# Scores of two units side by side on two row parts, keys kept once, and projections of one attention as 128 and 64 rows

## The chip, the cores and the metric

The kernel runs on one core of a Trainium2 chip. A core has five engines with queues of their own: TensorE (PE in the rows; its weight loads are listed as PEld), VectorE (DVE), ScalarE (ACT), GpSimd (POOL) and SyncE (SP), which here issues loads and stores. TensorE reads its operands from the on-chip memory (SBUF, 128 partitions) and writes to eight banks of PSUM, from which VectorE and ScalarE copy. The metric is the device time of one execution in microseconds; lower is better.

## What is computed

A model of several layers on 16 sequences of 102 tokens with 192 features, all in float32: tokens and words are embedded, then come attention 0 (with relative positions), a layer of slots, attention 1 behind a convolution, a routed expert layer, attention 2, an MLP, attention 3 and a second expert layer. The change bears on the attentions 0, 1 and 2, each with 12 heads. Attention 2 in the reference, with 64 features a head:

```python
x = layernorm(h)                                      # (16, 102, 192)
q, k, v = (split_heads(x @ w) for w in (w_q, w_k, w_v))   # each w: 192 x 768
scores = einsum('bhnd,bhmd->bhnm', q, k) / sqrt(64)
attn = softmax(scores, axis=-1)
h = h + merge_heads(einsum('bhnm,bhmd->bhnd', attn, v)) @ w_o + b_o
```

Attention 1 has queries, keys and values of 16 features a head. Attention 0 has queries and keys of 64 and values of 16, adds to the scores a product of the queries with position keys, shifted row by row, and divides alike.

## The kernel before

Each attention runs in four turns (a loop over NG = 4 groups of GB = 4 sequences). A turn first turns the normalized rows XN (`xt`, L1856 for its transposes) into XT, 96 features on the partitions in two parts; then come the projections to queries (QT), keys and values, and then the attention proper.

**Units.** A unit is three heads of one sequence; a turn has 16 units, and `attention` (L1905 and on, on TensorE) runs 23 steps. At step s TensorE does, in this order: the scores of unit s (L1929, three products of 102 x 102, into one bank), a third of an output projection of a finished sequence (L1941, in some steps from 10 on), the values of unit s - 5 (L1958), the transposes of the probabilities of unit s - 3 (L1968), and in attention 0 what stands beside (`pos`, position products L2019, or work of the next turn, L1856 and L2011).

**The round of a unit.** VectorE takes the minimum of the scores (L931; in attention 0 it first adds the positions, L925), ScalarE three exponentials with their sums (L1620), VectorE the reciprocals (L937), GpSimd the product of probabilities and reciprocals (L675), TensorE the transposes, ScalarE the copy to PT (L1614), TensorE the values, and when a bank of values is full VectorE copies it to OT (L947). VectorE's order at its step s is: the copy to OT of unit s - 6 if it filled a bank, the minimum of unit s, the reciprocals of unit s - 1. ScalarE's order is: PT of unit s - 4, exponentials of unit s, and in attention 0 what stands beside. A bank of values is full after two units in attention 2 and after four in the others.

**Banks.** Eight banks are dealt out by name. Outside attention 0, scores rotate over banks 0, 1 and 6 and values over 4 and 7; in attention 0, scores have 0 and 1 and values have 4, and 6 and 7 serve the work beside. A wait of TensorE for a bank of values is a wait for VectorE's copy to OT (`values_taken`).

**Keys in halves.** The scores use all 128 rows of a tile of QT, which holds the same three heads of two units (four in attention 1), one on each part of the rows. So that only one unit's rows count, KZ holds the keys once for each part with zeros in the other rows. GpSimd clears KZ ahead of each attention (L687, L762, L808), and ScalarE or VectorE copies each key tile in pieces: two of 64 rows in attention 0 (L1652 and L1653, or L1126 and L1127) and 2 (L1793, L1794), four of 32 rows in attention 1 (L1765).

**Projections of attention 2.** Each of 12 tiles of queries and keys and 8 of values is two products over 96 rows (`two`, `token_rows`, in `product`, L1838), with 408 columns for queries and keys (banks 6 and 7) and 384 for values (banks 4 and 5). Every float32 product shows as two records in the trace. VectorE normalizes the next turn's rows (`layernorm`, L881) while TensorE projects this one's.

## Time and profile before

| | us |
|---|---|
| median of three runs | 1664.0 (1656.38 to 1665.09) |
| the profiled execution, its own time | 1669.9 |
| its span | 1668.2 |
| TensorE busy in the span | 1421.3 |
| ScalarE busy | 657.6 |
| VectorE busy | 675.5 |
| GpSimd busy | 387.6 |

The profile is of one execution. A row of a time line gives the start in us from the start of the span, the length in us, the engine, the line of the kernel, the operation, what it writes and reads, and how many instructions were merged in the row; in brackets stands how long the engine was idle before it and what ended that. A matmul's length is more than its share of the engine, since matmuls are pipelined: starts are to be compared with starts. Attention 0 lies at 71 to 290 us, attention 1 at 633 to 815, attention 2 at 1052 to 1315.

### The profile page before, as it was taken

Reading aid. Unit: us, or ns where it says so; the run is one execution under the profiler, and the core shown is the slowest. Engines: PE = TensorE matmul, PEld = TensorE weight load, DVE = VectorE, ACT = ScalarE, POOL = GpSimd, SP = SyncE. Lnnn points to the kernel's source line nnn. Section 1 sums busy time; section 2 is a strip of 40 time slices with the busy share of each in tenths; the row PEclk is TensorE's granted clock in tenths of the full one; section 3 lists DMA queues with packets and bytes.
Section 4 is the critical chain, followed back from the end, with each engine's and each line's share of the span. In section 5 each row is a group of like instructions: output and inputs, shape, how many; then the busy total and the mean of one; then the engine's idle time right before and its main releaser. Section 6 shows DMA issues by size and latency. Waiting matters only on the chain.

```text
span 1668.2 us, 31119 instructions
## 1 busy us (share of the span) xinstructions
PE 1421.3 (85%) x10060; PEld 1047.2 (63%) x10060; DVE 675.5 (40%) x2110; ACT 657.6 (39%) x2225; POOL 387.6 (23%) x467
## 2 busy tenths in 40 slices
PE   5898887685678687888999899699999999989994
PEld 4556655552233355666668899375676776889994
DVE  5357667511101665444334422344343323451113
ACT  1477666230000335777642122255554542113331
POOL 5122223210000222222201365121121100024441
PEclk8699999567876698999999899799999999889997
DMA  7342432529996200000005464200000300136553
GB/s 221 92 130 72 129 86 73 232 92 417 415 416 208 77 1 1 1 0 0 1 0 142 147 197 147 67 2 0 0 0 0 133 0 0 41 96 189 186 170 106
DMA packets 98454, 178.71 MB, mean 107 GB/s; under 512 B 35434, under 2 KB 62344, under 8 KB 96720
## 3 DMA queue, kind: packets, MB, share of 16 engines
q1 hardware_dynamic: 84160, 130.65, 24.7%
q10 hardware_dynamic: 7056, 30.67, 4.5%
q0 software_dynamic: 7136, 16.10, 3.1%
q8 instruction: 56, 0.92, 0.2%
q14 instruction: 46, 0.38, 0.1%
HBM read 150.39 MB, written 26.99 MB: 106 GB/s over the span
## 4 chain that ended last, share of the span: by engine, by line
PE 58%; issue 12%; DVE 12%; DMA 8%; ACT 6%; SPq 2%; POOL 1%; DVEq 0%; ACTq 0%; POOLq 0%
PE bank L1838 15%; DMA WM<-in_fc 6%; PE bank L2355 6%; PE bank L2341 4%; PE bank L1929 4%; PE bank L1941 4%; PE bank L1958 3%; PE bank L2345 3%; PE bank L1968 3%; PE bank L2019 2%; PE bank L2011 2%; PE bank L1904 2%; ACT ON L1620 2%; PE bank L2272 2%; DVE MXU L931 1%
## 5 line engine op out<-in xcount | busy, mean ns | idle before, releaser
L1838 PE MATMUL bank<-XT,AREA 96*128 96x408 f32 (+1 forms) x640 | 240.4, 534 | 33.1 <-ACT XT L1574 15.8
L1838 PEld LDWEIGHTS bank<-XT,AREA 96*128 96x128 f32 (+1 forms) x640 | 122.4, 197 | 140.1 <-issue 100.8
L1929 PE MATMUL bank<-KZ,QT 128*102 128x102 f32 x1152 | 138.8, 259 | 8.7 <-ACT PB L1620 5.8
L675 POOL TENSOR_TENSOR PB<-PB,RCU 102x306 f32<-102x306 f32 x96 | 69.2, 720 | 329.4 <-DVE RCU L937 329.3
L659 POOL TENSOR_TENSOR RS<-VE,expo 102x4 f32<-102x4 f32 (+1 forms) x53 | 53.0, 1000 | 385.9 <-DVE VE L877 326.1
L1929 PEld LDWEIGHTS bank<-KZ,QT 128*102 128x102 f32 x1152 | 120.7, 172 | 26.3 <-issue 17.0
L2355 PE MATMUL bank<-WM,KZ 128*128 x660 | 118.2, 327 | 0.0
L2355 PEld LDWEIGHTS bank<-WM,KZ 128*128 128x128 f32 x660 | 105.7, 190 | 0.4
L1601 ACT ACTIVATE KZ<-bank,AREA 128x128 f32<-128x128 f32 x198 | 54.8, 376 | 121.7 <-PE bank L2345 121.7
L1958 PE MATMUL bank<-PT,VALL 102*32 102x102 f32 (+1 forms) x1152 | 85.3, 268 | 16.6 <-DVE OT L947 14.1
L1941 PE MATMUL bank<-AREA,OT 128*102 128x192 f32 x384 | 88.5, 344 | 11.1 <-DVE SLOTS L1292 5.3
L1614 ACT ACTIVATE PT<-bank 102x306 f32<-102x306 f32 x192 | 86.0, 450 | 26.2 <-PE bank L1968 25.7
L794 POOL DMA_INDIRECT rows_out<-KZ,TARGET x66 | 66.6, 1009 | 119.0 <-DVE KZ L1437 74.2
L675 POOL TENSOR_TENSOR ON<-ON,RCU 102x306 f32<-102x306 f32 x96 | 67.0, 698 | 90.8 <-DVE RCU L937 90.4
L1620 ACT ACTIVATE PB<-bank,MXU 102x102 f32<-102x102 f32 x192 | 65.8, 375 | 53.9 <-DVE MXU L931 53.8
L2341 PE MATMUL bank<-KZ,SLOTS 128*128 128x128 f32 x660 | 84.6, 275 | 2.6 <-issue 2.6
L2341 PEld LDWEIGHTS bank<-KZ,SLOTS 128*128 128x128 f32 x660 | 82.0, 192 | 3.4 <-issue 3.4
L1572 ACT ACTIVATE XT<-bank 96x408 f32<-96x408 f32 x56 | 25.9, 502 | 140.2 <-PE bank L1856 117.1
L782 POOL DMA_INDIRECT KZ<-rows_in,TOKEN x66 | 67.6, 1024 | 54.1 <-DVE TOKEN L1414 34.6
L931 DVE TENSOR_REDUCE MXU<-bank 102x3 f32<-102x306 f32 x128 | 61.0, 477 | 42.3 <-PE bank L1929 37.9
L1958 PEld LDWEIGHTS bank<-PT,VALL 102*32 102x32 f32 (+1 forms) x1152 | 43.1, 118 | 55.7 <-issue 33.9
L1838 PE MATMUL bank<-AREA,XT 96*102 96x192 f32 (+2 forms) x320 | 72.1, 377 | 0.0
(336 smaller groups left out, 2655.7 us busy)
## 6 DMA issues: line engine op xcount, KB each, us to landing
AREA<-in_fc SPq DMA_DIRECT2D x10, 1536.0 KB, 25.1
SLOTS<-in_m3w SPq DMA_DIRECT2D x33, 384.0 KB
WM<-in_fc ACTq DMA_DIRECT2D x5, 2304.0 KB, 14.0
WM<-in_fc SPq DMA_DIRECT2D x6, 1536.0 KB, 24.6
AREA<-in_fc ACTq DMA_DIRECT2D x4, 2304.0 KB, 14.4
SLOTS<-in_m1w SPq DMA_DIRECT2D x33, 256.0 KB
AREA<-pos_scratch SPq DMA_DIRECT2D x16, 459.0 KB
pos_scratch<-AREA SPq DMA_DIRECT2D x8, 913.5 KB
```

What stands on the lines that cost most here:

```text
L675: pool.tensor_tensor(p, p, scale, ALU.mult).then_inc(sem["probs_ready"], 1)
L782: pool.indirect_dma_start(XG[i % XRING], None, rows_in, bass.IndirectOffsetOnAxis(ap=TOKEN[:, i:i + 1], axis=0), bounds_check=NB * T - 1, ...
L794: pool.indirect_dma_start(rows_out, bass.IndirectOffsetOnAxis(ap=TARGET[:, i:i + 1], axis=0), YO[i % YRING], None, bounds_check=2 * NB * T ...
L931: give(dve.tensor_reduce(MXU[:, n % 4, 0:HPU], scores, AX.X, ALU.min), "probs_in")
L1614: free(activation(PT[s % 2][:, 0:HPU, :], src, ACT.Copy), k)
L1620: last = activation(p, p if pos else psum[k][0:T, cols(j)], ACT.Exp, scale=-1.0, bias=MXU[:, s % 4, j:j + 1], accum_out=SMU[:, s % 4, j:j ...
L1838: last = pe.matmul(dst, lhsT, rhs, start=n == 0, stop=n == len(pieces) - 1)
L1929: last = pe.matmul(psum[k][0:T, cols(j)], QT[:, tile, cols(bb)], KALL[:, unit % per_tile * (HEADS // per_tile) + tile, cols(bb)], start=Tr ...
L1941: last = pe.matmul(psum[PROJBANK][0:T, 0:D], OT[bb % 2][:, m, :], wo[:, m, :], start=m == 0, stop=m == parts - 1)
L1958: last = pe.matmul(psum[k][row:row + rows, cols(tile)], by_head(dv)[:, bb * HEADS + h, :], PT[n % 2][:, j, :], start=True, stop=True)
L2341: pe.matmul(p[:, c], w_all[:, (j * per + m) * 128:(j * per + m + 1) * 128], x[:, 0:TILE], start=m == 0, stop=False)
L2355: last = pe.matmul(p[:, 0:D], HG[i % HRING][:, f * 128:(f + 1) * 128], w2[:, bass.ds(e, 1), f * D:(f + 1) * D].rearrange("p o d -> p (o d) ...
```

## The change

**Scores.** At the end of every even step, behind values and transposes, TensorE computes the scores of units s and s + 1, their products in turns, one unit on one part of the rows and the other on the next (64 rows each in attentions 0 and 2, 32 in attention 1), into two banks. At odd steps there are none. Keys are kept once (KT); the pieces, the clearing of KZ and the waits for it are gone. Outside attention 0 the banks for scores are 0, 1, 6 and 7, those for values are bank 4 alone.

**Projections of attention 2.** The weights of queries, keys and values are loaded as 128 rows and, beneath, as the last 64 rows with one half of the columns on partitions 0 to 63 and the other on 64 to 127. VectorE writes the first 128 features of the normalized rows to XN and the last 64 twice side by side to TWICE, so that XT has 128 features in part 0 and the last 64 twice in part 1. Two tiles are made at a time: each gets a product over 128 rows and one over 64 rows, the two of 64 rows on different row parts, and from one pair of tiles to the next the order of 128 and 64 alternates. Queries and keys take four banks (2, 3, 6, 7), values four (0, 1, 4, 5). W2_LOADS becomes 20.

TensorE in the middle of attention 2, before (QT and KZ: queries and keys; PT: turned probabilities; OT: finished rows):

```order
L1958 MATMUL bank7<-PT0,VALL 64x102 [waits values_taken,bank_free2]
L1958 MATMUL bank7<-PT0,VALL 64x102 x2
L1968 MATMUL bank2<-ident,PB0 102x102 [waits bank_free2,probs_ready]
L1968 MATMUL bank2<-ident,PB0 102x102 x2
L1941 MATMUL bank5<-AREA,OT1 102x192 x2
L1958 MATMUL bank7<-PT1,VALL 64x102 [waits bank_free3]
L1958 MATMUL bank7<-PT1,VALL 64x102 x2
```

and the same place in the changed kernel, with scores in banks 6 and 7:

```order
L1965 MATMUL bank6<-KZ,QT 102x102 [waits exp_ready]
L1965 MATMUL bank7<-KZ,QT 102x102
L1965 MATMUL bank6<-KZ,QT 102x102
L1965 MATMUL bank7<-KZ,QT 102x102
L1965 MATMUL bank6<-KZ,QT 102x102
L1965 MATMUL bank7<-KZ,QT 102x102
L1996 MATMUL bank4<-PT0,VALL 64x102 [waits values_taken]
L1996 MATMUL bank4<-PT0,VALL 64x102 x2
L2006 MATMUL bank2<-ident,PB0 102x102 [waits bank_free2,probs_ready]
```

Scores now come by sixes ahead of the values of an odd step, and values go to bank 4 where they had 4 and 7 in turns.

VectorE in the changed kernel, around the copy to OT that those values wait for (its order is as before):

```order
L934 TENSOR_REDUCE MXU<-bank6 102x3 [waits scores_ready,sums_ready]
L940 RECIPROCAL RCU<-SMU 102x3 [waits exp_ready,probs_in]
L950 COPY OT0<-bank4 128x306 [waits values_ready,sums_ready]
L934 TENSOR_REDUCE MXU<-bank7 102x3 [waits scores_ready,values_taken]
L940 RECIPROCAL RCU<-SMU 102x3 [waits exp_ready,probs_in]
```

The copy stands between the minima of the two units of a pair.

The diff, cut to its core:

```diff
-W2_LOADS = 8 + 6
+W2_LOADS = 3 * 3 + 5 + 6
+SBANKS, TBANKS, OBANKS, XBANKS, FBANKS, VBANKS = (0, 1), (2, 3), (4, 5), (6, 7), (2, 3, 6, 7), (0, 1, 4, 5)
-        SCORES, VALUES = (SBANKS + XBANKS[:1], SBANKS), (OBANKS[:1] + XBANKS[1:], OBANKS[:1])
+        SCORES, VALUES = (SBANKS + XBANKS, SBANKS), (OBANKS[:1], OBANKS[:1])
...
-            pool.wait_ge(sem["gated"], at.now("gated") + CT3)
-            pool.wait_ge(sem["power_out"], at.now("power_out"))
-            pool.memset(KZ[:], 0.0).then_inc(sem["halves_cleared"], at.one("halves_cleared"))
-            pool.wait_ge(sem["halves_cleared"], at.now("halves_cleared"))
...
+            def layernorm_in_parts(src):
+                statistics(src)
+                power(ts(VE[:], MV[:, :, 1], EPS, None, ALU.add))
+                dve.wait_ge(sem["xn_taken"], at.now("xn_ready"))
+                for bb in range(GB):
+                    mean, scale = MV[:, bb, 0:1], RS[:, bb:bb + 1]
+                    ts(XN[:, bb, 0:128], src(bb)[:, 0:128], mean, scale, ALU.subtract, ALU.mult)
+                    last = ts(TWICE[:, bb, :].rearrange("t (two p) -> t two p", two=2),
+                              src(bb)[:, 128:D].unsqueeze(1).to_broadcast([T, 2, D - 128]),
+                              mean, scale, ALU.subtract, ALU.mult)
...
-                src = full(k)[:, 0:TG]
-                activation(KZ[0:64, 0, p, :], src[0:64], ACT.Identity, bias=bk0[0:64, p:p + 1])
-                free(activation(KZ[64:128, 1, p, :], src[64:128], ACT.Identity, bias=bk0[64:128, p:p + 1]), k)
+                free(activation(KT[:, p, :], full(k)[:, 0:TG], ACT.Identity, bias=bk0[:, p:p + 1]), k)
...
-                    src = full(k)[:, 0:TG]
-                    for u in range(UPB):
-                        rows = slice(32 * u, 32 * u + 32)
-                        last = activation(KALL[rows, 3 * u + j, :], src[rows], ACT.Identity,
-                                          bias=bqk1[rows, 3 + j:4 + j])
-                    free(last, k)
+                    free(activation(KT[:, j, :], full(k)[:, 0:TG], ACT.Identity, bias=bqk1[:, 3 + j:4 + j]), k)
...
+            def two_at_once(banks, shape, whole, half, n):
+                places = [claim(banks) for _ in range(2)]
+                last = [None, None]
+                for step in range(2):
+                    for j, (k, p) in enumerate(places):
+                        lhsT, rhs = (half if step == n % 2 else whole)(j)
+                        last[j] = pe.matmul(p[0:shape[0], 0:shape[1]], lhsT, rhs, start=step == 0, stop=step == 1)
+                        if step == 0 and j == 0:
+                            say_taken(last[j])
+                return [filled(ins, k) for ins, (k, p) in zip(last, places)]
...
-                for s in range(STEPS):
-                    if s < UNITS:
-                        bb, unit = s // UPB, s % UPB
-                        k = banks[s % len(banks)]
-                        if s < len(banks):
+                def scores_of_two(first):
+                    two_units = (first, first + 1)
+                    for n in two_units:
+                        if n < len(banks):
+                            k = banks[n]
                             pe.wait_ge(sem[f"bank_free{k}"], at.now(f"bank_full{k}") + 1)
                         else:
                             pe.wait_ge(sem[scores_read], at.take(scores_read))
-                        for j in range(HPU):
-                            tile = unit // per_tile * HPU + j
-                            last = pe.matmul(psum[k][0:T, cols(j)], QT[:, tile, cols(bb)],
-                                             KALL[:, unit % per_tile * (HEADS // per_tile) + tile, cols(bb)],
-                                             start=True, stop=True)
-                        last.then_inc(sem["scores_ready"], at.one("scores_ready"))
+                    for j in range(HPU):
+                        for n in two_units:
+                            bb, unit = n // UPB, n % UPB
+                            row = unit % per_tile * (128 // per_tile)
+                            rows, tile = slice(row, row + 128 // per_tile), unit // per_tile * HPU + j
+                            last = pe.matmul(psum[banks[n % len(banks)]][0:T, cols(j)], QT[rows, tile, cols(bb)],
+                                             KT[rows, tile, cols(bb)], start=True, stop=True)
+                            if j == HPU - 1:
+                                last.then_inc(sem["scores_ready"], at.one("scores_ready"))
...
+                    if s < UNITS and s % 2 == 0:
+                        scores_of_two(s)
...
-                xt()
+                xt_in_parts()
                 qk = []
-                for w in (wq2, wk2):
-                    for p6 in range(6):
-                        k, p = claim(XBANKS)
-                        qk.append(filled(product(p[:, 0:TG], two(w, p6 * 128, (p6 + 1) * 128)), k))
+                for n, w in enumerate((wq2, wk2)):
+                    for m in range(3):
+                        qk += tiles_at_once(w, m, 3 * n + m)
```

## Rows read from the trace of the kernel before

**Rows 1.** The page, part 1: busy us, share of the span, instructions.

```profile
PE 1421.3 (85%) x10060; PEld 1047.2 (63%) x10060; DVE 675.5 (40%) x2110; ACT 657.6 (39%) x2225; POOL 387.6 (23%) x467
```

**Rows 2.** Windows: a turn of attentions 0, 1, 2; PE, PEld, DVE, ACT, POOL busy, clock, DMA.

```profile
128.00:186.00 58.00, 51.49 (x412) 35.18 (x410) 41.69 (x111) 40.20 (x152) 13.92 (x18) 1.00 0.39 103
686.00:729.00 43.00, 37.74 (x312) 26.51 (x312) 18.88 (x58) 32.74 (x131) 12.15 (x17) 1.00 0.00 0
1126.00:1189.00 63.00, 59.78 (x379) 41.20 (x378) 26.84 (x74) 33.56 (x133) 12.15 (x17) 1.00 0.00 0
```

**Rows 3.** Time line of attention 2, TensorE and one minimum of VectorE.

```profile
1102.72 0.56 PE L1958 MATMUL bank<-PT,VALL 102*64 102x102 f32 x6
1103.22 0.47 PE L1968 MATMUL bank<-ident,PB 102*102 102x102 f32 x3
1103.53 0.70 PE L1929 MATMUL bank<-KZ,QT 128*102 128x102 f32 x6
1104.16 0.56 PE L1958 MATMUL bank<-PT,VALL 102*64 102x102 f32 x6
1104.34 0.48 DVE L931 TENSOR_REDUCE MXU<-bank 102x3 f32<-102x306 f32 x1
...
1105.51 0.82 PE L1941 MATMUL bank<-AREA,OT 128*102 128x192 f32 x4
1106.25 0.56 PE L1958 MATMUL bank<-PT,VALL 102*64 102x102 f32 x6
```

**Rows 4.** Time line of TensorE in the second expert layer.

```profile
1561.02 1.50 PE L2341 MATMUL bank<-KZ,SLOTS 128*128 128x128 f32 x12
1562.45 0.94 PE L2345 MATMUL bank<-KZ,SLOTS 64*128 64x128 f32 x12
1563.32 0.33 PE L2328 MATMUL bank<-ident,KZ 128*128 128x128 f32 x1
```

**Rows 5.** The chain of waits: start, us, what; the projections of attention 2.

```profile
1128.35 27.03 PE bank L1838 x80
```

**Rows 6.** Time line of attention 1: key copies and the first scores.

```profile
692.21 7.28 ACT L1765 ACTIVATE KZ<-bank,AREA 32x408 f32<-32x408 f32 x12 [0.77 <-PE bank L1838]
...
699.59 1.83 PE L1929 MATMUL bank<-KZ,QT 128*102 128x102 f32 x18 [0.67 <-issue]
```

**Rows 7.** Time line ahead of attention 1 and in its first turn.

```profile
633.02 5.24 DVE L881 TENSOR_SCALAR XN<-SLOTS,MV,RS 102x192 f32<-102x192 f32 x4 [1.12 <-POOL RS L659]
633.11 4.18 POOL L762 MEMSET KZ<- 128x4896 f32 x1
...
644.01 1.25 DVE L881 TENSOR_SCALAR XN<-SLOTS,MV,RS 102x192 f32 x4 [1.21 <-POOL RS L659]
```

**Rows 8.** Time line of attention 1: ScalarE and TensorE.

```profile
706.43 0.39 ACT L1620 ACTIVATE PB<-bank,MXU 102x102 f32<-102x102 f32 x1
...
706.64 0.38 PE L1958 MATMUL bank<-PT,VALL 102*32 102x102 f32 x6
...
707.39 0.49 ACT L1614 ACTIVATE PT<-bank 102x306 f32<-102x306 f32 x1
...
707.94 0.38 PE L1958 MATMUL bank<-PT,VALL 102*32 102x102 f32 x6
```

**Rows 9.** Attention 0: waits of PE (us in total, times, longest); time line around one.

```profile
PE bank L1958 <- DVE OT L947: 14.1, 8, 3.6
...
153.84 0.47 DVE L947 COPY OT<-bank 128x306 f32<-128x306 f32 x1
...
154.36 0.38 PE L1958 MATMUL bank<-PT,VALL 102*32 102x102 f32 x6 [0.61 <-DVE OT L947]
```

**Rows 10.** Time line of attention 0: scores of units 11 and 15, and position copies.

```profile
159.12 0.78 PE L1929 MATMUL bank<-KZ,QT 128*102 128x102 f32 x6
...
160.35 0.88 ACT L1662 ACTIVATE AREA<-bank 102x406 f32<-102x406 f32 x2
...
170.28 0.78 PE L1929 MATMUL bank<-KZ,QT 128*102 128x102 f32 x6
```

More of the change, by code:

```diff
@@ L375, in build @@
         a2(KD, 2, NB * T)
-        wq2, wk2, wv2 = a2(KD, 2, FF), a2(KD, 2, FF), a2(KD, 2, FF)
+        wq2, wk2, wv2 = ((a2(128, FF), a2(128, HALF_F)) for _ in range(3))
         wo2, bo2 = a2(128, 6, D), a2(T, D)
@@ L416, in build @@
                "second_loaded", "biases_loaded", "gelu_loaded",
-               "y_ready", *(f"y_loaded{g}" for g in range(NG)), "moe_done", "halves_cleared", "values_ready", "values_taken", "scaled",
+               "y_ready", *(f"y_loaded{g}" for g in range(NG)), "moe_done", "values_ready", "values_taken", "scaled",
                "attn0_done", "attn1_done",
@@ L684, in _ @@
             powers(1)
-            pool.wait_ge(sem["power_out"], at.now("power_out"))
-            for half in range(2):
-                pool.memset(KZ[64 - 64 * half:128 - 64 * half, half, :, :], 0.0
-                            ).then_inc(sem["halves_cleared"], at.one("halves_cleared"))
-            pool.wait_ge(sem["halves_cleared"], at.now("halves_cleared"))
             words(NB // 2, NB, "words_behind")
@@ L804, in _ @@
             expert_rows(1)
-            for r in range(YRING):
-                pool.wait_ge(sem[f"scattered{r}"], 16 * len(range(r, TILES, YRING)))
-            for half in range(2):
-                pool.memset(KZ[64 - 64 * half:128 - 64 * half, half, :, :], 0.0
-                            ).then_inc(sem["halves_cleared"], at.one("halves_cleared"))
-            pool.wait_ge(sem["halves_cleared"], at.now("halves_cleared"))
             powers(1)
@@ L886, in layernorm @@
                     step(last)
+            def layernorm_in_parts(src):
[8 more added lines that the diff above has]
+                              mean, scale, ALU.subtract, ALU.mult)
+                give(last, "xn_ready")
+                dve.wait_ge(sem["xn_ready"], at.now("xn_ready"))
             xn = lambda bb: XN[:, bb, :]
@@ L957, in attention, with values @@
                         between(s)
-            def values(v, dv, bias):
+            def values(v, dv, bias, banks=OBANKS):
                 per = 2 * D // dv
@@ L963, in values @@
                 for first in range(0, GB * HEADS, per):
-                    k = at.bank(OBANKS)
+                    k = at.bank(banks)
                     src = full(k)[0:T, 0:per * dv].rearrange("p (h d) -> p h d", d=dv)
@@ L1785, in _ @@
             with at.loop(act, NG) as g:
-                turned(XT)
-                for p in range(6):
-                    k = at.bank(XBANKS)
+                turned(XTALL)
+                for p in (0, 3, 1, 4, 2, 5):
+                    k = at.bank(FBANKS)
                     free(activation(QT[:, p, :], full(k)[:, 0:TG], ACT.Copy, scale=-0.125), k)
-                for p in range(6):
-                    k = at.bank(XBANKS)
-                    src = full(k)[:, 0:TG]
-                    activation(KZ[0:64, 0, p, :], src[0:64], ACT.Copy)
-                    free(activation(KZ[64:128, 1, p, :], src[64:128], ACT.Copy), k)
+                for p in (0, 3, 1, 4, 2, 5):
+                    k = at.bank(FBANKS)
+                    free(activation(KT[:, p, :], full(k)[:, 0:TG], ACT.Copy), k)
                 attention()
@@ L1871, in xt, with xt_in_parts, tiles_at_once, values_at_once @@
                 fresh.append(True)
+            def xt_in_parts():
+                pe.wait_ge(sem["xn_ready"], at.take("xn_ready"))
+                out = []
+                for part in (XN[:, :, 0:128], TWICE):
+                    k, p = claim(XBANKS)
+                    for bb in range(GB):
+                        last = pe.transpose(p[:, cols(bb)], part[:, bb, :], ident[0:T, 0:T])
+                    out.append(filled(last, k))
+                moved(*out)
+                fresh.append(True)
+            def two_at_once(banks, shape, whole, half, n):
[8 more added lines that the diff above has]
+                return [filled(ins, k) for ins, (k, p) in zip(last, places)]
+            def tiles_at_once(w, m, n):
+                whole, half = w
+                rows = lambda j: slice(64 * j, 64 * j + 64)
+                return two_at_once(FBANKS, (128, TG),
+                                   lambda j: (whole[:, j * HALF_F + m * 128:j * HALF_F + (m + 1) * 128], XTALL[:, 0, :]),
+                                   lambda j: (half[rows(j), m * 128:(m + 1) * 128], XTALL[rows(j), 1, :]), n)
+            def values_at_once(w, bb):
+                whole, half = w
+                rows = lambda j: slice(64 * j, 64 * j + 64)
+                return two_at_once(VBANKS, (T, HALF_F),
+                                   lambda j: (XTALL[:, 0, cols(bb)], whole[:, j * HALF_F:(j + 1) * HALF_F]),
+                                   lambda j: (XTALL[rows(j), 1, cols(bb)], half[rows(j), :]), bb)
             def two(w, n0, n1, x=XT):
@@ L2254, in _ @@
             convolution_out(1)
-            zeros_there(1)
             with at.loop(pe, NG) as g:
```

36 lines of the change are left out of this document (15 added, 21 removed).

## The prediction

> **What bounds the kernel now.** I read the page first [rows 1]: TensorE (PE) is busy for 85% of the span, ScalarE (ACT) for 39%. That is a mean over many stages, so I next cut out one turn of each of the three attentions [rows 2]. In attention 2 TensorE is busy for 60 of 63 us, in attention 1 for 38 of 43, in attention 0 for 51 of 58. ScalarE is busy for 34, 33 and 40. So attention 2 is bound by TensorE, attention 1 nearly as much by ScalarE, and attention 0 by both and the waits between them. Nothing else in the program is touched, so only these three stages (four turns each) and what stands ahead of them can move the time.
>
> Then the time line of TensorE for one unit of attention 2 [rows 3]. The reader is to see that the starts lie end to end: values 1102.72, transposes 1103.22, scores 1103.53, so 0.50, 0.31 and, up to the next values at 1104.16, 0.63: one unit in 1.44 us. An output projection adds 0.65, from 1105.51 to 1106.25 less the 0.09 by which scores end sooner where no values follow.
>
> **What the pairs save, part by part.** *Rows side by side.* The experts already run halves of 64 rows in pairs [rows 4]: twelve records of full rows take 1.43 us to the next line, twelve of 64 rows 0.87, the way back to full rows in it. For a change between full and part rows I take the 0.09 that scores show above when values follow. Scaled from 128 columns to 102, two units' scores cost 0.77 with both changes; I take 0.82, since the first weights of a block show. Before they cost 2 x 0.63. Gain on TensorE: 0.4 us a pair.
>
> *Projections of attention 2.* Before: 80 records in 27.03 us a turn [rows 5], 0.338 each. After: of every eight records four are full and four run in two places at once, so 60 steps, 20.3; five blocks of half rows with some 0.3 each for both changes make 21.8, and 0.2 goes to the first weights. Gain 5.0 a turn, 20.1 in all; bounds 0 (no overlap) and 27 (no price for changes). ScalarE's copies (0.5 each against 2.2 a pair) and VectorE's hide. The two last value copies now end together, so the first minimum is 0.4 later: +1.6.
> The Trainium skill (TensorEngine Tiling (Array Packing), Theoretical Speedup) gives up to 2x for 64 rows; by that the projections would take 20.3 a turn and the sum would be 7 us lower. No run here shows a pair of 408 columns.
>
> *Keys copied once.* In attention 1 the twelve copies of 32 rows hold ScalarE for 7.28 us from 692.21, and scores, which wait for the last, start at 699.59 [rows 6]. With three copies of 0.6 TensorE sets the pace: from 692.21 two more key tiles of four records at 0.34 (2.7), then values, 16 records of half the columns (2.6), so scores start near 697.5. Gain 2.1 a turn, 8.5. In attention 2 nothing (TensorE sets the pace there). In attention 0 each key tile is copied in 0.6 rather than 1.2; of that 0.75 a turn shows, 3 us.
>
> *Clearing of KZ.* Ahead of attention 1 the memset (4.18) lies on the normalization, which takes 5.24 instead of 1.25 [rows 7]: gain 4.0. Ahead of attention 0 it lies on it too, but TensorE is then held by the position keys, so I take 2 for that start with its first keys. Ahead of attention 2 it runs while the rows are loaded: 0. The normalization there is cut in eight instructions rather than four: +0.7 once. The six more loads are issued far ahead: 0.
>
> **What the pairs cost.** *The turn of the loop.* Before, scores of unit s stand at the start of step s, and the values of unit s-3 come two steps later, behind the scores of s+2: three units per round. Now scores of s and s+1 stand at the end of step s, behind transposes, and the next pair must wait for values of s-3 in step s+2. ScalarE copies PT of s-3 only after the exponentials of s. So one round of two units is: end of the scores to the minimum 0.11 (1104.23 to 1104.34), minimum 0.48 [rows 3], exponentials 0.96 (706.43 to 707.39), PT to values 0.55 [rows 8], 2.1 in all; then values 0.31 (their row has 0.38 where 0.56 stands for 0.50 in attention 2) and transposes 0.31 with 0.09 for the change, and the pair itself, 0.78 up to the end of its row: 3.6 us for two units, 1.8 a unit where attention 1 now takes 1.30 (706.64 to 707.94).
>
> *One bank for values.* Scores now own banks 6 and 7, values bank 4 alone. The values of the next fill wait until VectorE has copied the last one, and VectorE's order puts that copy behind the minimum of the new pair and a reciprocal. Attention 0 has one bank already and shows the wait: eight times, 14.1 us in all, and values start 0.05 after the copy ends [rows 9]. In attention 2, which fills a bank every two units, the round is 0.11 + 0.48 + 0.03 + 0.18 + 0.03 + 0.48 + 0.05 = 1.36 from the end of scores to values, then 0.50 + 0.40 + 0.50 + 0.40 + 0.78: 3.94 for two units, where 2 x 1.44 = 2.88 go now. Queued behind that wait on TensorE are transposes and all later scores.
> The Trainium skill (TensorEngine Tiling (Array Packing), Gotcha 1: PSUM Pressure) says that different row tiles cannot write to one bank at a time; this kernel's pairs keep to that, and pay with the bank that values lose.
>
> *Sum for attention 2.* Start-up: PT of unit 1 waits for the exponentials of unit 4, whose scores now stand a step later, so pair 6 comes an estimated 0.9 later than score 7 now. Four rounds from pair 6 to pair 14: 4 x 3.94 + 3 projections that nothing hides x 0.65 = 17.7, where eight units and four projections take 14.1: +3.6. Tail, with one copy waited for: +0.8. Together +5.3 a turn, +21.2. *Attention 1*: start-up +1.1; four rounds at 3.6 with two bank waits that add 0.3 each, 15.0, where three units at 1.30 and five at 1.58 (1.25 of TensorE and 0.33 for half a projection) make 11.8 now: +3.2; tail +0.5: +4.8 a turn, +19.2. *Attention 0*: the pace is set by ScalarE's position copies (0.88 a unit, [rows 10]) and TensorE's position products, which wait for them; scores are now 2.8 apart there (159.12 to 170.28 for four units). A round of two units with a position product in it comes to 5.5: 2.1 less PT's 0.55, plus 0.5 for VectorE's added pass, 0.15 for longer exponentials and the 0.88, is 3.1; product 0.9; values, transposes, pair 1.5. That is 2.8 a unit, as now. But the last two position products stand one pair later, some 2 us a turn. Bounds -3.7 (8 pairs x 0.46, all on the path) and +5; I take +2, nearest to the rounds: +8.
>
> **Sum.** Attention 0: 8 - 3 - 2 = +3. Attention 1: 19.2 - 8.5 - 4.0 = +6.7. Attention 2: 21.2 + 1.6 - 20.1 + 0.7 = +3.4. Together +13. The profiled execution took 1669.9 (span 1668.2), so 1683 by it; the median of the three runs is 1664.0, 6 below, and I give the time against that: **1677**.
>
> **Rivals.** *ScalarE sets the pace (faster).* If neither round binds because the next scores go ahead of the waits, attention 2 gains 0.4 x 8 pairs x 4 = 13, attention 1 falls to ScalarE's 1.30 a unit and gains 5 in its projection steps, attention 0 nothing; with -3 - 2 - 8.5 - 4 - 20.1 + 2.3 that is -53: 1611. For it: TensorE is the fuller engine [rows 2]. Against: TensorE takes its instructions in order, and the values that wait stand ahead of the scores. It decides where both rounds are below 2.6 us for two units.
> The Trainium skill (TensorEngine Tiling (Array Packing), PSUM Bottleneck) has that case: once tiling speeds up the matmuls, the copies out of PSUM become the bound; by that rule the rounds would be ScalarE's 1.30 a unit.
> *Attention 0 gains (no change).* Scores for two units in one block take one of two score blocks out of its chain. At -2 a turn rather than +2 the sum is -3: 1661. For it: its start-up, where the chain runs 2.9 a unit now, would be 2.5. Against: the late position products.
> *Halves do not overlap at 408 columns (slower).* The pairs seen have 128 columns. With no overlap the projections gain nothing: 1677 + 20 = 1697. Against: the time of the 128-column pair is mostly streaming. It decides at the first projection of attention 2.
> *The granted clock falls in the attentions (slower).* With waits of 1.4 us in every round the 1.00 of [rows 2] may not hold; scores, values and transposes at half speed for a quarter of the stages give some +30: 1707.
>
> **How the numbers follow.** Forecast 0.57, ScalarE's pace 0.12, attention 0 gains 0.18, no overlap 0.08, clock 0.05. The forecast's own range is 1668 to 1692 (rounds 0.3 us a unit off either way in part of the units, projections 4 us off). The range 1655 to 1697 takes in the no-change case and the end of the no-overlap case and leaves out ScalarE's pace, the clock and tails. About 0.5% (8 us) is what a measurement of this kernel tells from no change. Slower: most of the forecast, both slow rivals: 0.59. Same: most of attention 0's case and the forecast's lower end: 0.25. Faster: 0.16.
>
> **What would show it.** In the profile after: idle time of TensorE before values put down to the copy into OT, in attention 2 about 1.2 us at every second unit; in attention 1, values that wait for PT and a unit in 1.7 to 1.8; scores of a pair in 0.8; the projection stretch of attention 2 near 21.8; the normalization ahead of attention 1 at 1.3. Wrong it would be if a unit of attention 2 takes 1.5 or less in its middle, or if values never wait for the copy.

## The result: 7% slower, and where the time went

The changed kernel takes 1781.5 us in the median, the kernel before 1664.6 beside it: a ratio of 1.070 (95% interval 1.065 to 1.075), some 117 us. I had forecast 13 us, in a range up to 1697. The sign was right and the size was not. Executions of one kernel spread by up to 2.5% here, and the profiled ones of the runs named single and order_only are 1.5 to 1.8% above their fastest, so of these two I read single turns with their clock beside them.

First the page of the profile: TensorE's busy time and the granted clock of TensorE in 40 slices (tenths of full speed), of the changed kernel,

```profile
PE 1465.8 (83%) x10060; PEld 1047.1 (59%) x10060; DVE 663.9 (37%) x2114; ACT 617.7 (35%) x2153; POOL 374.9 (21%) x462
PEclk9887885577786895666598899779779799989997
```

and the row of the clock of the kernel before, which I had not quoted:

```profile
PEclk8699999567876698999999899799999999889997
```

TensorE runs as many instructions as before [rows 1] and is busy 44 us longer. The attentions lie at slices 2 to 7, 15 to 20 and 26 to 33: before, the clock there is nearly all nines; after, it is fives to nines. The windows of one turn of attentions 0, 1 and 2 (start and end, length, busy us of PE, PEld, DVE, ACT, POOL, clock, share and rate of DMA) say how much, to be read against [rows 2]:

```profile
122.20:190.30 68.10, 60.09 (x409) 38.44 (x408) 39.46 (x108) 38.52 (x149) 13.92 (x18) 0.77 0.33 88
719.80:781.00 61.20, 51.45 (x315) 32.17 (x314) 18.90 (x58) 28.18 (x121) 12.14 (x17) 0.61 0.00 0
1236.10:1307.90 71.80, 60.54 (x378) 38.75 (x376) 27.73 (x78) 30.32 (x127) 12.15 (x17) 0.83 0.00 0
```

A turn grew from 58 to 68 us, from 43 to 61, from 63 to 72, at a clock of 0.77, 0.61 and 0.83 where it had been 1.00. Scores of a pair in attention 1 last 1.36 us at the half clock (at 729.58) and 0.79 at the full one (at 721.42 in the run named fill).

The waits that I had forecast are there too. Waits of TensorE in attention 1 (us in total, times, longest):

```profile
PE bank L2006 <- POOL PB L679: 12.4, 8, 2.6
PE bank L1996 <- DVE OT L950: 11.4, 8, 1.4
PE bank L1996 <- ACT PT L1615: 7.2, 8, 0.9
```

L2006 are the transposes: they wait for GpSimd's product of probabilities at the start of each turn, behind the first two pairs (2.6 and 0.5 us in the first turn). L1996 are the values, L950 is the copy to OT, L1615 the copy to PT. In attention 2 the copy to OT holds TensorE for 20.8 us in 21 waits. And where attention 2 runs at the full clock for a moment, a round of a pair can be read (TensorE's time line):

```profile
1194.03 0.79 PE L1965 MATMUL bank<-KZ,QT 64*102 64x102 f32 x12
1196.25 0.56 PE L1996 MATMUL bank<-PT,VALL 102*64 102x102 f32 x6 [1.44 <-DVE OT L950]
1196.75 0.47 PE L2006 MATMUL bank<-ident,ON 102*102 102x102 f32 x3
1197.50 0.90 PE L1979 MATMUL bank<-AREA,OT 128*102 128x192 f32 x4 [0.28 <-DVE H L1500]
1198.33 0.56 PE L1996 MATMUL bank<-PT,VALL 102*64 102x102 f32 x6
...
1199.22 0.79 PE L1965 MATMUL bank<-KZ,QT 64*102 64x102 f32 x12
```

Pair to pair it is 5.19 us; less the projection (0.83) and its own wait (0.28), 4.08.

### The profile page after: what moved, and what is told of

The parts are those of the page before. It is cut to its first block, busy times and chain, and to the rows that moved or that the text cites. A ratio compares the mean times of both kernels' runs of the same rounds, so it can differ in the third digit from the quotient of the medians.

```text
span 1774.9 us, 31077 instructions
## 1 busy us (share of the span) xinstructions
PE 1465.8 (83%) x10060; PEld 1047.1 (59%) x10060; DVE 663.9 (37%) x2114; ACT 617.7 (35%) x2153; POOL 374.9 (21%) x462
## 4 chain that ended last, share of the span: by engine, by line
PE 42%; issue 31%; DVE 9%; DMA 7%; ACT 4%; POOL 4%; SPq 1%; POOLq 0%; DVEq 0%; ACTq 0%
PE bank L2390 6%; PE bank L2376 4%; PE bank L1830 4%; PE bank L1965 3%; DMA WM<-in_fc 3%; DMA KZ<-in_fc 3%; PE bank L2380 3%; PE bank L2006 3%; PE bank L1979 3%; PE bank L1996 3%; PE bank L2058 2%; PE bank L2050 2%; POOL PB L679 1%; DVE MXU L934 1%; PE bank L1884 1%
## 5 line engine op out<-in xcount | busy, mean ns | idle before, releaser
L1830 PE MATMUL bank<-XT,AREA 96*128 96x408 f32 (+1 forms) x448 | 171.7, 543 | 24.5 <-ACT XT L1575 15.1
L1996 PE MATMUL bank<-PT,VALL 102*32 102x102 f32 (+1 forms) x1152 | 111.8, 337 | 62.2 <-DVE OT L950 51.1
L1830 PEld LDWEIGHTS bank<-XT,AREA 96*128 96x128 f32 (+1 forms) x448 | 87.7, 200 | 99.5 <-issue 74.1
L1996 PEld LDWEIGHTS bank<-PT,VALL 102*32 102x32 f32 (+1 forms) x1152 | 54.4, 144 | 129.2 <-issue 55.0
L1979 PE MATMUL bank<-AREA,OT 128*102 128x192 f32 x384 | 118.0, 431 | 10.8 <-DVE H L1500 4.8
L1965 PE MATMUL bank<-KZ,QT 64*102 64x102 f32 (+1 forms) x1152 | 103.4, 333 | 0.8 <-DVE ON L928 0.8
L1965 PEld LDWEIGHTS bank<-KZ,QT 64*102 64x102 f32 (+1 forms) x1152 | 85.6, 229 | 19.5 <-issue 12.4
L1615 ACT ACTIVATE PT<-bank 102x306 f32<-102x306 f32 x192 | 81.6, 427 | 34.3 <-PE bank L2006 33.7
L1979 PEld LDWEIGHTS bank<-AREA,OT 128*102 128x102 f32 x384 | 72.7, 222 | 30.6 <-issue 12.1
L1621 ACT ACTIVATE ON<-bank,MXU 102x102 f32<-102x102 f32 x192 | 64.2, 351 | 69.6 <-DVE MXU L934 69.6
L2006 PE MATMUL bank<-ident,PB 102*102 102x102 f32 x288 | 60.7, 336 | 25.9 <-POOL PB L679 25.9
```

What stands on the lines that cost most here:

```text
L1615: free(activation(PT[s % 2][:, 0:HPU, :], src, ACT.Copy), k)
L1621: last = activation(p, p if pos else psum[k][0:T, cols(j)], ACT.Exp, scale=-1.0, bias=MXU[:, s % 4, j:j + 1], accum_out=SMU[:, s % 4, j:j ...
L1830: last = pe.matmul(dst, lhsT, rhs, start=n == 0, stop=n == len(pieces) - 1)
L1965: last = pe.matmul(psum[banks[n % len(banks)]][0:T, cols(j)], QT[rows, tile, cols(bb)], KT[rows, tile, cols(bb)], start=True, stop=True)
L1979: last = pe.matmul(psum[PROJBANK][0:T, 0:D], OT[bb % 2][:, m, :], wo[:, m, :], start=m == 0, stop=m == parts - 1)
L1996: last = pe.matmul(psum[k][row:row + rows, cols(tile)], by_head(dv)[:, bb * HEADS + h, :], PT[n % 2][:, j, :], start=True, stop=True)
```

## Experiments

The first question was how much of the loss is clock and how much is waits; the second, what brings the clock down.

### fill: the waits are kept, and filled

```diff
+                    fill = 0 if pos or s % 2 == 0 or not 3 <= s < UNITS else 30 if s == 3 else 10
+                    if fill:
+                        tk, tp = claim(TBANKS)
+                        for _ in range(fill):
+                            pe.transpose(tp[0:T, cols(0)], ident[0:T, 0:T], ident[0:T, 0:T])
                     n = s - 5
...
-                        k, p = claim(TBANKS)
+                        k, p = (tk, tp) if fill else claim(TBANKS)
```

> The changed kernel with more work for TensorE: in attentions 1 and 2, at odd steps, ten transposes of the identity (thirty at step 3) into the bank that the step's own transposes overwrite later, ahead of the values that wait. Nothing waits less. Theory (the clock): the waits of the pair's round make the granted clock fall to a half, and that is most of the loss; with the idle time filled the clock stays at 1.0, a turn of attention 1 falls from 61 to 47 to 50 us, one of attention 2 from 72 to 64 to 67, and the whole to 1690 to 1725 although TensorE does more. Rival (the waits alone): the clock has no part, or falls for another reason; the added work hides in the waits or lengthens the rounds: 1780 to 1810.

Measured: 1717.8 us, ratio 1.029 (1.026 to 1.032): 64 us come back by giving TensorE more to do. Windows of a turn of attention 1 and of 2:

```profile
712.80:760.50 47.70, 42.25 (x403) 30.18 (x402) 18.91 (x58) 28.04 (x121) 12.15 (x17) 1.00 0.00 0
1185.40:1250.70 65.30, 60.60 (x468) 40.86 (x466) 27.73 (x78) 30.16 (x127) 12.15 (x17) 1.00 0.00 0
```

90 more records in each turn, the clock at 1.00, and the turn 13.5 and 6.5 us shorter. Now the rounds can be read at the full clock, in attention 2:

```profile
1197.14 0.56 PE L2001 MATMUL bank<-PT,VALL 102*64 102x102 f32 x6 [0.43 <-DVE OT L950]
...
1198.93 0.79 PE L1965 MATMUL bank<-KZ,QT 64*102 64x102 f32 x12
1199.65 1.08 PE L1987 MATMUL bank<-ident 102*102 102x102 f32 x10
1201.16 0.56 PE L2001 MATMUL bank<-PT,VALL 102*64 102x102 f32 x6 [0.43 <-DVE OT L950]
```

4.02 us for two units; I had forecast 3.94. In attention 1 a round without a projection takes 3.48 (values at 719.67 and 723.15); forecast 3.6.

### fill_all: attention 0 filled as well

The condition on `pos` is dropped for the ten (the thirty at step 3 stay out of attention 0).

> The changed kernel with ten added transposes at every odd step of all three attentions, ahead of the values (thirty at step 3 of attentions 1 and 2): the filled kernel of the earlier run, with attention 0 filled as well. If the clock in attention 0 (0.77 to 0.82, a turn of 66 to 68 us) is what is left of the loss there, its turns fall to 58 to 62 us and the whole from 1718 to 1690 to 1705. Rival: the late position products and waits make it, or the added work stands in their way: turns of 66 to 70, 1715 to 1730.

Measured: 1695.1 us, ratio 1.019 (1.012 to 1.025). Turns of attention 0 take 59.5, 63.8 and 60.9 us, at a clock of 0.97, 0.92 and 0.97 (before: 0.96, 1.00 and 0.97). So at about the clock of before the change costs some 30 us, and some 86 of the 117 (1781.5 less 1695.1) come back with the clock; the added work has its own small price in what is left.

### rows_only: one size, in the kernel before

```diff
-                            last = pe.matmul(psum[k][0:T, cols(j)], QT[:, tile, cols(bb)],
-                                             KALL[:, unit % per_tile * (HEADS // per_tile) + tile, cols(bb)],
+                            row = unit % per_tile * (128 // per_tile)
+                            rows = slice(row, row + 128 // per_tile)
+                            last = pe.matmul(psum[k][0:T, cols(j)], QT[rows, tile, cols(bb)],
+                                             KALL[rows, unit % per_tile * (HEADS // per_tile) + tile, cols(bb)],
```

> The kernel before with one size changed and no instruction moved: the scores' products read only the rows of the queries and keys that count (64 in attentions 0 and 2, 32 in attention 1) where they read all 128, zeros in the others. Keys, clearing, banks, order and projections are those of before. Theory (the clock follows the rows that are used): with waits as few as before the granted clock falls in the attentions as it did with single units, to 0.6 to 0.75, a turn of attention 1 grows from 43 to some 58 us, one of attention 2 from 63 to some 80, and the whole comes to 1800 to 1880 us. Rival (waits alone make the clock fall): the clock stays at 0.97 and the time within 15 us of 1664.

Measured: 1916.2 us, ratio 1.158 (1.149 to 1.167), the slowest kernel of all, though no instruction moved, and slower than the theory had it (1800 to 1880). A turn of attentions 1 and 2, a stretch of each with the lower clock, and what TensorE waits for in the four turns of attention 2:

```profile
758.60:824.50 65.90, 60.66 (x313) 39.61 (x313) 18.89 (x58) 34.71 (x130) 12.16 (x17) 0.61 0.00 0
1307.90:1391.10 83.20, 79.88 (x378) 54.05 (x377) 26.83 (x74) 34.56 (x133) 12.17 (x17) 0.75 0.00 0
694.40:748.90 54.50, 52.35 (x260) 33.47 (x260) 16.26 (x51) 25.24 (x107) 11.86 (x17) 0.50 0.00 1
1226.80:1271.20 44.40, 44.26 (x210) 32.71 (x210) 12.01 (x35) 19.84 (x97) 10.47 (x16) 0.50 0.00 1
```
```profile
PE bank L1931 <- ACT PB L1620: 4.8, 4, 1.2
PE bank L1943 <- DVE H L1499: 4.3, 4, 1.1
PE bank L1838 <- ACT XT L1572: 2.9, 4, 0.8
PE bank L1970 <- POOL PB L675: 1.2, 4, 0.4
```

In the kernel before, the same four stretches show:

```profile
PE bank L1941 <- DVE H L1499: 4.3, 4, 1.1
PE bank L1929 <- ACT PB L1620: 3.2, 4, 0.8
PE bank L1838 <- ACT XT L1572: 2.1, 3, 0.7
PE bank L1968 <- POOL PB L675: 1.7, 5, 0.3
```

TensorE waits for nothing new in attentions 1 and 2 (in attention 2 the lines above sum to 13.2 us in four turns, 11.3 before), and yet the granted clock is at its lower level (0.50, that is 1.2 GHz) for most of the loop over the units: 54.5 of the 67.3 us of the first turn of attention 1, 44.4 of the 84.6 of the first of attention 2. In attention 0 three turns run at 0.87, 0.77 and 0.56 (60.3, 68.0 and 82.3 us), while its waits for the copy to OT fall from 14.1 [rows 9] to 5.0 us. The zeros in KZ had been no waste: scores over all 128 rows went with the full clock, and they take no longer (0.63 from one unit's scores to the values behind them [rows 3], and 0.63 on 64 rows at the full clock in the run named single).

### order_only: the pairs' place and banks, over all 128 rows

Into the kernel before go the loop `scores_of_two` at the end of even steps and the banks of the changed kernel; the products read `QT[:, ...]` and `KALL[:, ...]` with the zeros.

> The kernel before with the pairs' place and banks alone: at the end of every even step the scores of units s and s + 1, banks 0, 1, 6, 7 for scores and 4 for values, but over all 128 rows with the zeros, clearing, four copies of keys and the old projections. It has the waits of the changed kernel without its part rows. Theory (rows hold the clock): the granted clock stays near 1.0 in attentions 1 and 2; only the waits cost, a turn of attention 1 is 47 to 50 us, of attention 2 66 to 69, attention 0 0 to 5 a turn more, the whole 1695 to 1725. Rival (the waits bring the clock down by themselves): clock below 0.85 there and 1750 to 1800 us.

Measured: 1786.7 us, ratio 1.074 (1.066 to 1.082). Neither alternative held: the theory had the clock of attentions 1 and 2 nearly right and the price of the waits too low, the rival had the whole right and that clock wrong. A turn each of attentions 0, 1 and 2:

```profile
142.40:208.40 66.00, 57.37 (x411) 39.34 (x410) 41.59 (x111) 40.30 (x152) 13.95 (x18) 0.90 0.35 91
759.90:810.90 51.00, 37.45 (x313) 26.27 (x313) 18.89 (x58) 33.33 (x130) 12.16 (x17) 1.00 0.00 0
1260.20:1330.50 70.30, 59.88 (x378) 40.78 (x377) 26.83 (x74) 33.45 (x133) 12.16 (x17) 1.00 0.00 0
```

In attentions 1 and 2 the clock is at 1.00 in one of the first three turns and at 0.91 and 0.93 in the other two, which are 3.5 to 4 us longer: there the waits alone touch it little, against 0.59 to 0.75 in rows_only. The waits cost 7.7 and 7.5 us a turn at the full clock (against 43.3 and 62.8 before); a pair over all rows has no saving to set against them. In attention 0 the clock is 0.77 to 0.90: there the waits bring it down without part rows.

### single: part rows, no pairs

One unit's scores at a time at the head of the step, on `QT[rows]` and `KT[rows]`, with the banks of before; the rest as changed.

> The changed kernel with the scores of one unit at a time again, at the head of the step, on one row part of the keys kept once, and with the banks of before (0, 1, 6 for scores, 4 and 7 for values in attentions 1 and 2). Keys once, no clearing and the new projections of attention 2 stay. Theory: all of the loss is in the pairs at the end of the even steps (their waits, and the clock that falls with them). Then what is left are gains: projections 27.0 to 23.8 us a turn, 13 us; keys of attention 1 some 8; the clearing ahead of attention 1 4 and ahead of attention 0 up to 15; together 1625 to 1640 us, granted clock near 0.97 in all three attentions. Rival: reading keys and queries on row parts, or the projections and loads, cost something by themselves: then it stays above 1664.

Measured: 1833.2 us (1797 to 1843), slower than with pairs. My theory for this run was wrong, and it was the run that pointed to the rows. A turn of attention 1 and of attention 2:

```profile
737.20:798.10 60.90, 57.42 (x313) 38.11 (x312) 18.91 (x58) 29.20 (x121) 12.14 (x17) 0.64 0.00 0
1261.80:1341.00 79.20, 74.96 (x378) 49.97 (x376) 27.74 (x78) 31.07 (x127) 12.14 (x17) 0.74 0.00 0
```

TensorE is busy for 57 of 61 and 75 of 79 us, at 0.64 and 0.74 of its clock. In attention 0, on 64 rows too, the first three turns run at 0.56, 0.97 and 0.64, so there the clock is not settled by the rows alone.

### copyfirst: VectorE's copy ahead of the new pair's minimum

```diff
-                    n = s - 6
+                    n = s - 5
                     if 0 <= n < UNITS and av_filled(dv, n % UPB):
```

> The changed kernel with one thing moved: VectorE copies a full bank of values to OT ahead of the minimum of the new pair instead of behind it and a reciprocal. Theory of the one bank: the wait for that copy makes the round; without it a turn of attention 2 falls by 6 to 10 us, of attention 1 by some 4, the whole to 1725 to 1750. Rival (the turn of the loop): the next wait, of the odd step's second values for PT behind the exponentials of the new pair, takes its place nearly at once; rounds keep their length and the whole stays at 1765 to 1785.

Measured: 1756.5 us, ratio 1.053 (1.049 to 1.058), between the two forecasts. The waits for the copy fall from 20.8 to 0.7 us in attention 2 and disappear in attention 1; waits for PT (2.1 to 4.0 and 7.2 to 8.2 us) and for the projections' bank (4.8 to 10.8 and 4.3 to 9.7) take part of their place. The clock moves with the waits (0.83 to 0.87 in attention 2), so this run does not part bank and loop.

### ahead: pairs out of the way of the waits

```diff
-                    if s < UNITS and s % 2 == 0:
-                        scores_of_two(s)
+                    if not pos and s % 2 == 0 and s + 2 < UNITS:
+                        scores_of_two(s + 2)
```

In attention 0 one unit at a time (on 64 rows), and VectorE's copy between minimum and reciprocal.

> Keys once and the new projections as in the changed kernel; attention 0 with one unit's scores at a time at the head of the step; in attentions 1 and 2 pairs, but a pair earlier: units s + 2 and s + 3 at the end of even step s (0 and 1 at the start), and VectorE copies the full bank between the minimum and the reciprocal of its step. Theory: the pairs lose only by their place; ahead of the waits they cost 0.8 us for two units against 2 x 0.63, so against the kernel with one unit at a time it gains some 3 us a turn in attention 2 and 0 to 1 in attention 1, 10 to 16 us in all: 1612 to 1628. Rival: the single bank of values, or the other engines' pace, binds still; then it is as the one with single units or slower, with waits for the copy in the trace.

Measured: 1728.9 us, ratio 1.036 (1.033 to 1.039), 100 us above my theory. The waits for the copy are gone (0.7 us for OT in attention 2); what is left is a wait of the third pair for the exponentials, once a turn, 11.7 us in four in attention 2 and 9.8 in attention 1. The clock is not back:

```profile
729.10:783.40 54.30, 49.80 (x315) 31.64 (x314) 18.90 (x58) 28.74 (x121) 12.14 (x17) 0.62 0.00 0
1213.30:1275.80 62.50, 57.24 (x378) 37.08 (x376) 27.74 (x78) 30.91 (x127) 12.14 (x17) 0.89 0.00 0
```

### proj_only and proj_early: the other parts alone

proj_only is the kernel before with the projections of attention 2 changed, and nothing else. proj_early also moves one clearing:

```diff
-            powers(1)
-            pool.wait_ge(sem["power_out"], at.now("power_out"))
             for half in range(2):
                 pool.memset(KZ[64 - 64 * half:128 - 64 * half, half, :, :], 0.0
                             ).then_inc(sem["halves_cleared"], at.one("halves_cleared"))
             pool.wait_ge(sem["halves_cleared"], at.now("halves_cleared"))
+            powers(1)
```

> The kernel before with the projections of attention 2 alone changed (128 and 64 rows by pairs of banks, rows normalized in two parts, twenty loads); scores, keys and clearing are those of before. From the changed kernel's trace, where that stretch takes 23.8 us at the full clock against 27.0: 3.2 a turn less, 12.8, with the last value copies 0.4 a turn later: some 1653 us (1648 to 1658). My prediction had 21.8 for the stretch: 1646. Rival (rows and clock): halves of 64 rows bring the clock down there or in the scores behind them: 1664 or more.

Measured: 1650.2 us, ratio 0.994 (0.990 to 0.998). TensorE's time line there:

```profile
1123.90 14.02 PE L1911 MATMUL bank<-XT,AREA 64*128 64x408 f32 x48 [0.93 <-ACT XT L1591]
1137.76 8.62 PE L1911 MATMUL bank<-AREA,XT 64*102 64x384 f32 x32
1146.30 1.86 PE L1988 MATMUL bank<-KZ,QT 128*102 128x102 f32 x18
```

22.4 us for the 80 records that took 27.0 [rows 5], at the full clock: halves do overlap at 408 columns, and here products on part rows leave the clock at 1.00. The 23.8 us of my expectation are the first turn of the changed kernel, at a clock of 0.91; its second, at 1.00, takes 22.1.

> The one above, and GpSimd clears the key halves of attention 0 before it makes the first reciprocal root instead of behind it, so that the clearing does not lie on the first normalization (5.04 us against 1.40 in the changed kernel). If the missing wait of TensorE there keeps the clock at 1.0 in the first projections, as in the changed kernel (first scores at 55.6 against 70.9 us), it gains 10 to 15 us more: 1638 to 1645. If the clearing then holds up VectorE's work before the normalization as long, 0 to 3 us: 1650.

Measured: 1636.6 us, ratio 0.986 (0.981 to 0.991): 14 us less than proj_only. Scores begin at 60.0 us instead of 70.8, and the first turn of attention 0 takes 56.7 us instead of 61.9, at a clock of 0.97 instead of 0.87. A turn of attention 1 and of attention 2 for what follows:

```profile
687.80:731.10 43.30, 37.75 (x313) 26.57 (x313) 18.94 (x59) 32.95 (x130) 12.14 (x17) 1.00 0.00 0
1133.50:1192.60 59.10, 55.22 (x378) 36.81 (x376) 27.71 (x78) 33.29 (x133) 12.15 (x17) 1.00 0.00 0
```

### ahead_fill4, 8 and 2: a version that beats both

proj_early, and in attentions 1 and 2 the pairs ahead with keys once and no clearing, with added transposes at odd steps (`4`, `8` or `2`) and thirty ahead of the third pair:

```diff
+                    fill = 0 if pos else 30 if s == 2 else 4 if s % 2 and 5 <= s < UNITS else 0
+                    if fill:
+                        held = claim(TBANKS)
+                        for _ in range(fill):
+                            pe.transpose(held[1][0:T, cols(0)], ident[0:T, 0:T], ident[0:T, 0:T])
```

> Attention 0 as before, with all rows and zeros, cleared early, and the new projections of attention 2; attentions 1 and 2 with keys once, nothing cleared, pairs one pair ahead of their place (as in the run named ahead) and added transposes: thirty ahead of the third pair at the start of a turn, four at each odd step from 5 to 15. Against the kernel with the projections and the early clearing alone (1636.6): if four are enough to hold the clock at 1.0, a turn of attention 1 is 39 to 42 us instead of 43.2 and one of attention 2 57 to 60 instead of 59.2, and 4 us of clearing go: 1610 to 1632. If not, the turns are 50 to 54 and 61 to 64 as in ahead: 1665 to 1685.

Measured: 1625.5 us, ratio 0.977 (0.971 to 0.983), the fastest kernel here: 2.3% ahead of the kernel before. Turns of attentions 1 and 2:

```profile
672.80:714.00 41.20, 38.57 (x369) 27.03 (x368) 18.88 (x58) 27.73 (x121) 12.17 (x17) 1.00 0.00 0
1118.90:1178.50 59.60, 56.67 (x434) 37.65 (x432) 27.71 (x78) 30.56 (x127) 12.17 (x17) 1.00 0.00 0
```

Against proj_early (1636.6) the turn of attention 1 is 2.1 us shorter, which is what keys copied once save there, and that of attention 2 is 0.5 longer. From the normalization ahead of attention 1 to its first scores it is 14.3 us instead of 23.3. By these numbers what this kernel gains over proj_early comes with the keys and the clearing that is gone; the pairs themselves, with the transposes that they need, are not shown to gain anything.

> The one above with eight added transposes at each odd step. More of them hold the clock more surely, at up to 0.4 us a pair where TensorE sets the pace, 2.4 us a turn: at the full clock 41 to 44 and 59 to 63 us a turn, 1625 to 1650. If the clock falls all the same: 1670 to 1690.

Measured: 1647.9 us, ratio 0.989 (0.983 to 0.996), turns 43.2 and 61.7 at 1.00: the added work shows.

> The kernel with four added transposes at each odd step, with two. From eight to four a turn of attention 1 fell from 43.2 to 41.2 us and one of attention 2 from 61.7 to 59.6, both at the clock 1.0. If two still hold the clock: some 40.2 and 58.6, the whole 1615 to 1622. If the clock falls to a half in the middle of the turns, as it does in the run named ahead with none: 44 to 54 and 60 to 64, 1640 to 1685.

Measured: 1647.7 us, ratio 0.988 (0.982 to 0.994). Two turns of attention 1 in a row and one of attention 2:

```profile
632.10:687.10 55.00, 52.70 (x355) 34.51 (x354) 18.92 (x58) 28.63 (x121) 12.16 (x17) 0.66 0.00 1
687.10:727.70 40.60, 37.79 (x356) 25.99 (x356) 18.90 (x58) 27.55 (x121) 12.17 (x17) 1.00 0.00 0
1142.50:1201.10 58.60, 55.67 (x420) 36.60 (x418) 27.73 (x78) 30.20 (x127) 12.16 (x17) 1.00 0.00 0
```

The same instructions take 55.0 us in one turn and 40.6 in the next. Two hold the clock in attention 2, in attention 1 in every second turn; four hold it in all turns of both.

## Why the prediction was wrong, step by step

Cut where a normalization starts, the two traces differ by 106.7 us. Beside it stand my terms and the same cut of fill_all, where the clock is near 1.0:

| stretch | forecast | after | fill_all |
|---|---|---|---|
| up to the first scores of attention 0 | -2 | -15 | -16 |
| on to the normalization ahead of attention 1 | +5 | +29 | +16 |
| on to that ahead of attention 2 | +7 | +62 | +15 |
| to the end | +3 | +30 | +8 |
| together | +13 | +107 | +23 |

So the sign was not luck: with the clock about as before, fill_all is still 27 us slower than the kernel before. But its three later stretches cost 39 us, with the added transposes in them, where I had 15, and the start gained 16 where I had 2; these two errors partly cancel.

- **The step that failed** is the sum itself: every duration in it is one at the full clock, from rows of a kernel whose clock was 1.00 [rows 2], so the clock stood in it at nothing. A falling clock was my last rival, with 0.05 and +30 us. Its price was too low (some 86 us), and its cause was wrong for the most part: I put it to the waits. Waits alone take the clock to 0.77 to 0.90 in attention 0 and leave it at 0.91 to 1.00 in attentions 1 and 2 (order_only); products that read part of the rows take it to 0.59 to 0.75 in attentions 1 and 2 without new waits (rows_only), and in attention 0 as well. The edit that I booked as a gain of 0.4 us a pair was the one that took most of the clock.
- **The rounds** were right: 4.02 to 4.08 us against 3.94 in attention 2, 3.48 against 3.6 in attention 1. A turn at the full clock came to 47.7 us (46.0 by my terms) and 65.3 (63.5); the added transposes are in these. The start-up was too small: I had +1.1 and +0.9, and in the changed kernel the first transposes of a turn of attention 1 wait 3.1 us, where the kernel before waits some 1.0 there.
- **Projections of attention 2**: 22.1 to 22.4 us against 21.8 and 0.2 for first weights, a gain of 4.5 to 4.8 a turn (from start to start it was 26.85) against 5.0. Right for the stretch; of the 4.6 that I had left of it behind the later first minimum, the turn of attention 2 shows 3.7 (62.8 to 59.1 in proj_only).
- **Keys copied once**: from the first projection to the first scores of attention 1 it was 13.1 us (686.46 to 699.59) and is 11.0 (708.80 to 719.80): 2.1, as forecast. The normalization ahead of attention 1 takes 1.25 us again, as forecast [rows 7].
- **Clearing ahead of attention 0** was mis-sized: 2 us forecast, 15 measured. VectorE's normalization with the clearing beside it, in the kernel before,

```profile
28.75 5.04 DVE L1071 TENSOR_SCALAR XN<-H,MV,RS 102x192 f32<-102x192 f32 x4 [1.15 <-POOL RS L659]
28.78 4.33 POOL L687 MEMSET KZ<- 64x2448 f32 x2
```

and without it, in the changed one:

```profile
28.30 1.40 DVE L1074 TENSOR_SCALAR XN<-H,MV,RS 102x192 f32<-102x192 f32 x4 [1.15 <-POOL RS L663]
```

What I had missed is that the clock, at 0.50 from 34.6 to 72.1 us before, is at 1.00 from 28.3 to 59.0 after, so that the projections in between run at twice the clock. proj_early shows it alone: 14 us by moving the clearing alone. Without the delay the clock there stays at 1.00 up to 53.6 us, where in proj_only TensorE waits 2.8 us for the normalization and the clock is at 0.50 from 35.6 us on.

- **Attention 0's turns**: +2 forecast for the waits; at a clock of 0.92 to 0.97 they are 1.3 to 5.6 longer (fill_all against 58.2).
- **The rivals.** ScalarE's pace did not come: it needed rounds below 2.6 us. No overlap at 408 columns is refuted by proj_only. That attention 0 gains is refuted by its turns of 65 to 68 us, and by those of 59.5 to 63.8 in fill_all, where the clock is at 0.92 or more.

The Trainium skill (TensorE: Matmul & The Clock Gate, What's actually happening) has the gate set by how busy TensorE has been. The filled kernels agree. In rows_only the busy share of a turn of attention 2 is 96%, before 95%, and the clock 0.75 against 1.00. Part of these 96% is the slower clock itself, but the waits hardly grew (13.2 against 11.3 us in four turns): there the measurement decides, and it takes the rows that a product reads to tell the two kernels apart.

What stays open: why part rows lower the clock (their number, the zeros' part in it, and the weight loads, which read fewer rows too, were not tried apart), and how 64 rows compare with 32 by themselves, since attention 1 and 2 differ in other ways too. Nor do part rows always lower it: the projections of attention 2 in proj_only keep 1.00 with half of their records on 64 rows, and ahead_fill4 keeps it with pairs on part rows and added transposes. The finding is for these loops of small products.

## What to carry to other kernels

Before a product is cut to the rows that count, look at the clock of its stretch: where it is 1.00, as here, the zero rows cost a single product no time (0.63 us either way) and may be what keeps it there. Work out forecasts of an edit to TensorE at both levels of the clock, and where a new wait or smaller products come in, try a few idle transposes in the wait as the first experiment: here it parted clock and waits in one run. Pairs that stand behind the instructions that wait came with a loss in every run; ahead of them, with four added transposes, they come out about even (ahead_fill4 against proj_early), and a gain of their own is not shown.

## What the runs showed of the hardware

- The same instruction stream with scores of 64 and 32 rows instead of 128: 1916 against 1664 us, clock 0.59 to 0.61 against 1.00 in attention 1, at nearly unchanged waits.
- Added work made it faster: 90 more records a turn took a turn of attention 1 from 61.2 to 47.7 us.
- It is an edge: with two added transposes a step, neighbouring turns of one loop took 55.0 and 40.6 us; with four, all took 41.2.
- A clearing by GpSimd beside a normalization by VectorE (5.04 against 1.40 us) cost 14 us in the end (proj_early against proj_only), most of it with the clock of the projections behind it, which is at 0.50 with the delay and 1.00 without.
